# Softmax attention in a decoder kernel: the mask goes from TensorE to VectorE, and copies move from VectorE to ScalarE and GpSimd

## The chip, the cores and the metric

The kernel runs on one core of a Trainium2 chip. The metric is the device time of one launch in microseconds: the median of 3 runs is 2063.61 us (2063.49 to 2066.27). One further launch was recorded by the hardware profiler and is read below. Its engines are TensorE (PE in the rows; PEld are its weight loads), VectorE (DVE), ScalarE (ACT), GpSimd (POOL) and SyncE (SP), which issues transfers.

## The reference

A decoder of six sublayers works on 16 sequences of 128 tokens and 512 features. Each sublayer's result is added to x and layer-normed. The change touches the first and the fifth, both softmax attention over 16 heads of 32 features:

```python
# first: grouped queries (4 heads of k and v), rotary q and k
scores = jnp.einsum('btkgd,bskd->bkgts', qg, k) * scale
mask = jnp.tril(jnp.ones((T, T), dtype=scores.dtype))
scores = scores + mask[None, None, None]
p = jax.nn.softmax(scores, axis=-1)
out = jnp.einsum('bkgts,bskd->btkgd', p, v).reshape(B, T, C)
return out @ wo.T + bo
# fifth: causal, k and v from 128 latent features
scores = jnp.einsum('bhqd,bhkd->bhqk', qh, kh) * inv_sqrt_d
scores = jnp.where(causal, scores, jnp.finfo(scores.dtype).min)
attn = jax.nn.softmax(scores, axis=-1)
out = jnp.einsum('bhqk,bhkd->bhqd', attn, vh)
return out @ Wout.T
```

So in both a mask that is the same for all heads is added to 128 by 128 scores of each head: 0 and 1 in the first, 0 and a very low number in the fifth. The others are an attention over latents, a ternary feed-forward, a decayed attention without softmax and one with experts.

## The kernel before

`attention_phase` writes the code of the first ("gqa"), the fourth ("decay") and the fifth ("causal") sublayer; `soft` is true for the two with softmax, which run from about 10 to 270 us and from about 1297 to 1531 us of the profiled execution. A "batch" is one sequence: its 128 tokens are the 128 partitions. Products whose inputs need more exactness than one pass gives are made of three matmuls (L97 to L99): each factor is split into a rounded high part, written by ScalarE, and a low part, the difference.

The order of work is a list, `plan`, of events (name, batch, half or part). Each engine walks through that list and does its share of each event, so its order is fixed when the program is written; `act_plan` is ScalarE's own version of the list. The events are:

- S: the scores of a batch, all 16 heads in four PSUM banks. Before them TensorE writes the mask into each bank by a matmul with the identity (L857), and the scores are added to it (L866). For each half h (8 heads) VectorE takes the negated maximum (`nb`, L714) and ScalarE the exponentials out of PSUM into `pr`, with their sums (L572).
- T: TensorE turns the 8 probabilities' tiles of a half (L875), VectorE copies them to `pt` (L726).
- rec and rt: VectorE takes the reciprocals of the sums (L729), GpSimd spreads them over 512 columns (`spread`, L479), TensorE turns that (L880), ScalarE copies it to `rts` (L588).
- pv: probabilities by v (L891). VectorE multiplies the result by `rts` into `on` (L732), and ScalarE copies that to the high part `oth` (L592).
- lo: VectorE subtracts `oth` from `on` into the low part `otl` (L738).
- out: the output projection of `oth` and `otl` (12 matmuls), added to X by VectorE (L744), which then takes the statistics for the norm (L215 to L219). GpSimd makes the inverse root (L482).
- x, c, q, k, v: the turned inputs and the projections of the next group of 4 batches, split up over the "slots" of this group (two slots a batch, one in the middle of each of its halves). x and c have a high part by ScalarE (L540) and a low part by VectorE (L684); q, k and v are copied by VectorE (L688, L699, L704 or L710).
- mag: ScalarE sums absolute weights for the third sublayer (L578, first stage only); kr: a split for the second.

Projections, rt, pv and out share two PSUM banks in turn, so each needs the bank of the one before last to be copied out. TensorE's order in one batch b is: mask and scores of b, the first slot, T of half 1 of b-1, out of b-2, rt of b-1, the second slot, T of half 0 of b, pv of b-1. The last four batches have no slots to fill, since there is no next group.

## Time and profile before

| | |
|---|---|
| median of 3 runs | 2063.61 us |
| the profiled execution | 2068.66 us |
| its span, first to last instruction | 2066.9 us |
| mean granted TensorE clock | 0.97 |
| TensorE busy | 1886.0 us, 91% |
| VectorE busy | 1052.3 us, 51% |
| ScalarE busy | 708.4 us, 34% |
| GpSimd busy | 346.9 us, 17% |

A timeline row gives the start in us from the span's start, the duration in us, the engine, the line, the operation with output<-input, and in brackets how long the engine stood idle ahead of it and what ended that. Matmuls overlap in TensorE's pipeline, so the distance between starts says what one costs and the duration is longer. A wait for several things is put down to the last.

### The profile page before, as it was taken

The page shows a single profiled execution, that of the slowest core. Times are in us where ns is not written, and L with a number is a line of the kernel's source. Part 1 is how long each engine was busy: PE and PEld are TensorE (multiplying, and loading weights), DVE is VectorE, ACT ScalarE, POOL GpSimd, SP SyncE. Part 2 cuts the span into 40 slices and gives each one's busy share as a digit, 9 for nine tenths or more (in the row PEclk, how much of TensorE's full clock was granted, in tenths as well). Part 3 has the DMA queues.
Part 4 walks back from the last instruction along what each step waited for, and adds up shares of the span by engine and source line. Part 5 has one row for each costly group of instructions (what it writes and reads, how often), then busy time and mean ns, then how long its engine had stood idle before and what let it go on. Part 6 is the DMA issues. An engine that isn't in the chain of part 4 may idle for free. (4 is left out here: it accounts for less than half of the span.)

```text
span 2066.9 us, 32715 instructions
## 1 busy us (share of the span) xinstructions
PE 1886.0 (91%) x12124; PEld 1533.9 (74%) x12124; DVE 1052.3 (51%) x1852; ACT 708.4 (34%) x2276; POOL 346.9 (17%) x307
## 2 busy tenths in 40 slices
PE   8899888999999989999989999899979999999990
PEld 6666576788888867777767777677658877999990
DVE  4666854455455446433364457577765333222226
ACT  3555724344443332212141111455552121233322
POOL 1111100000000018100020010001103200735225
PEclk9999999999999999999999999899999999999995
DMA  7110143000000013000084000100013300643246
GB/s 240 43 40 21 43 149 95 1 1 1 1 1 1 1 55 114 1 0 0 0 314 181 1 1 32 42 1 1 1 47 126 129 1 16 239 165 126 76 128 193
DMA packets 65566, 135.83 MB, mean 66 GB/s; under 512 B 6672, under 2 KB 24976, under 8 KB 63376
## 3 DMA queue, kind: packets, MB, share of 16 engines
q1 hardware_dynamic: 41616, 96.24, 13.4%
q0 software_dynamic: 5840, 27.92, 3.9%
q10 hardware_dynamic: 17968, 9.71, 1.8%
q8 instruction: 96, 1.57, 0.3%
q14 instruction: 46, 0.38, 0.1%
HBM read 90.60 MB, written 43.25 MB: 65 GB/s over the span
## 5 line engine op out<-in xcount | busy, mean ns | idle before, releaser
L1472 PE MATMUL banks<-ternary_xth,ternary_wq 128*128 (+1 forms) x352 | 140.6, 399 | 5.0 <-DVE ternary_wq L1403 3.7
L1472 PE MATMUL banks<-ternary_xtl,ternary_wq 128*128 (+1 forms) x352 | 139.4, 396 | 0.0
L97 PE MATMUL banks<-latent_vh,latent_cth 128*128 128x512 f32 x256 | 104.2, 407 | 3.5 <-DVE latent_ctl L1173 3.5
L97 PE MATMUL banks<-weights,expert_xgh 128*128 x312 | 104.4, 335 | 2.3 <-DVE expert_xgl L2074 2.3
L572 ACT ACTIVATE gqa_pr<-banks,gqa_nb 128x128 f32<-128x128 f32 x256 | 90.1, 390 | 32.8 <-DVE gqa_nb L714 32.8
L99 PE MATMUL banks<-weights,expert_xgl 128*128 x312 | 101.2, 324 | 0.0
L98 PE MATMUL banks<-weights,expert_xgh 128*128 x312 | 101.1, 324 | 0.0
L572 ACT ACTIVATE causal_pr<-banks,causal_nb 128x128 f32<-128x128 f32 x256 | 90.0, 395 | 31.3 <-DVE causal_nb L714 31.2
L98 PE MATMUL banks<-latent_vl,latent_cth 128*128 128x512 f32 x256 | 100.3, 392 | 0.0
L99 PE MATMUL banks<-latent_vh,latent_ctl 128*128 128x512 f32 x256 | 100.1, 391 | 0.0
L1432 DVE TENSOR_TENSOR ternary_hf<-ternary_sg,banks 128x512 f32<-128x512 f32 x44 | 30.2, 687 | 135.4 <-issue 79.5
L1126 ACT ACTIVATE latent_pt<-banks 128x1024 f32<-128x1024 f32 x32 | 32.9, 1027 | 189.1 <-PE banks L1272 189.1
L1373 ACT ACTIVATE ternary_sg<-banks 128x512 f32<-128x512 f32 x44 | 26.3, 598 | 192.3 <-PE banks L1472 192.3
L1117 ACT ACTIVATE latent_pr<-banks,latent_nb 128x128 f32<-128x128 f32 x256 | 90.2, 373 | 0.0
L97 PE MATMUL banks<-latent_xgh,latent_ch 128*128 128x256 f32 x256 | 77.9, 304 | 9.4 <-DVE latent_xgl L1167 4.6
L1472 PEld LDWEIGHTS banks<-ternary_xth,ternary_wq 128*128 128x128 f32 x352 | 67.3, 191 | 23.2 <-DVE ternary_xtl L70 4.1
L1087 POOL TENSOR_TENSOR latent_rs<-latent_ve,mhalf 128x1 f32<-128x1 f32 x15 | 8.3, 550 | 445.8 <-DVE latent_ve L219 445.8
L1173 DVE TENSOR_TENSOR latent_ctl<-banks,latent_cth 128x512 fp32r<-128x512 f32 x64 | 42.9, 689 | 71.5 <-ACT latent_cth L1104 71.5
L1484 PE MATMUL banks<-ternary_wq,ternary_hh 128*128 128x512 f32 x176 | 70.9, 403 | 8.1 <-DVE ternary_hl L1436 5.8
L1472 PEld LDWEIGHTS banks<-ternary_xtl,ternary_wq 128*128 128x128 f32 x352 | 67.3, 191 | 14.2
L2082 DVE TENSOR_TENSOR expert_hf<-expert_sg,banks 128x352 f32<-128x352 f32 x39 | 20.4, 522 | 107.8 <-PE banks L99 107.8
L98 PE MATMUL banks<-latent_xgl,latent_ch 128*128 128x256 f32 x256 | 72.9, 285 | 0.0
(463 smaller groups left out, 5375.3 us busy)
## 6 DMA issues: line engine op xcount, KB each, us to landing
x_slots<-decay_zeros SPq DMA_DIRECT2D x39, 256.0 KB
y_slots<-decay_zeros SPq DMA_DIRECT2D x39, 256.0 KB
y_slots<-expert_ys SPq DMA_DIRECT2D x39, 256.0 KB
expert_xin<-x_slots SPq DMA_DIRECT2D x38, 256.0 KB, 2.9
weights_raw<-in_expert_experts SPq DMA_DIRECT2D x4, 2176.0 KB, 9.7
gqa_tw<-in_ternary_w ACTq DMA_DIRECT2D x4, 2112.0 KB
ternary_raw<-in_ternary_w SPq DMA_DIRECT2D x11, 768.0 KB, 4.3
expert_raw<-in_expert_experts POOLq DMA_DIRECT2D x3, 2176.0 KB, 9.8
```

Source lines behind the costliest of these rows:

```text
L97: pe.matmul(out, wh, xh, start=first, stop=False, **kw)
L98: pe.matmul(out, wh, xl, start=False, stop=False, **kw)
L99: return pe.matmul(out, wl, xh, start=False, stop=last, **kw)
L572: a = act.activation(pr[:, h, c, :], S.bank[2 * h + c // 4][:, (c % 4) * P:(c % 4 + 1) * P], ACT.Exp, bias=nb[:, h, c:c + 1], accum_out=su ...
L1117: a = act.activation(pr[:, c, :], S.bank[x][:, j * P:(j + 1) * P], ACT.Exp, bias=nb[:, c:c + 1], accum_out=sums[:, c:c + 1])
L1126: act.activation(pt[:, :, :], pair(1), ACT.Copy).then_inc(pt_done, 1)
L1173: dve.tensor_tensor(ctl[:, x, :], S.bank[2 + x], f32(cth[:, x, :]), ALU.subtract).then_inc(ct_lo, 1)
L1373: act.activation(sg[:, j % 2, :], gate[j % 2][:, :], ACT.Sigmoid).then_inc(sig_done, 1)
L1432: dve.tensor_tensor(hf[:, j % 2, :], sg[:, j % 2, :], up[j % 2][:, :], ALU.mult).then_inc(hf_done, 1)
L1472: a = pe.matmul(dst[:, :], wq[:, j, m, c * P:(c + 1) * P], x[:, c, toks], start=c == 0 and n == 0, stop=c == C - 1 and n == 1)
L1484: a = pe.matmul(yb[i][:, :], h[:, j % 2, i * P:(i + 1) * P], wq[:, j, 2, :], start=j == 0 and n == 0, stop=j == J - 1 and n == 1)
L2082: dve.tensor_tensor(hf[:, i % 2, :], sg[:, i % 2, :], up[i % 2][:, 0:F1], ALU.mult).then_inc(hf_done, 1)
```

## The change

In the two softmax stages:

1. The mask matmuls go, and with them `maskr` and `identr` and ScalarE's two copies that made them. VectorE adds the mask while it moves the scores of a half from PSUM to `pr` in SBUF (a 128x1024 addition, `masked`), and takes the maximum from there; ScalarE takes the exponentials in place in `pr`. TensorE's next scores wait for `masked` instead of for the exponentials.
2. T and rt of b-1 come directly behind the scores of b, ahead of the first slot; out of b-2 keeps its place between the slots. (In batch 1 they come behind the first slot.) The reciprocals come first in VectorE's batch.
3. ScalarE copies the second half's turned probabilities (`pt_late`), q, and in the fifth stage the even parts of v; its list has T and rt ahead of the exponentials, and the copies of a first slot's q or v between the two halves' exponentials.
4. The low part of the attention's output is made by GpSimd instead of VectorE. In the list it stands ahead of the spreading of the next batch's reciprocals.
5. In a batch with x in its first slot, and in batch 1, the second half's scores stay behind that slot.

```diff
@@ buffers @@
-            maskr, identr = sb("maskr", [P, P], F32R), sb("identr", [P, P], F32R)
+            mask = (S.tril if kind == "gqa" else S.causal)[:, :].unsqueeze(1).broadcast_to((P, 8, P))
@@ plan @@
         for b in range(B + 2):
             for h in range(2):
+                if soft and h == 0 and b >= 2:
+                    plan.append(("lo", b - 2, 0))
+                if soft and h == 0 and 1 <= b <= B:
+                    plan.append(("rec", b - 1, 0))
                 if b < B and (h == 0 or not soft):
                     plan.append(("S", b, h))
-                if soft and h == 0 and b >= 2:
-                    plan.append(("lo", b - 2, 0))
+                with_x = b % GT == 0 and b < B - GT
+                turned = [("T", b - 1, 1), ("rt", b - 1, 0)] if soft and h == 0 and 1 <= b <= B else []
+                if b != 1:
+                    plan += turned
+                if soft and h == 0 and b < B and not with_x and b != 1:
+                    plan.append(("S", b, 1))
                 if b < B - GT:
                     plan += [(n, b // GT + 1, i) for n, i in by_slot[2 * (b % GT) + h]]
...
+                if b == 1:
+                    plan += turned
-                if soft and h == 0 and b < B:
+                if soft and h == 0 and b < B and (with_x or b == 1):
                     plan.append(("S", b, 1))
...
-                    if h == 0 and 1 <= b <= B:
-                        plan += [("T", b - 1, 1), ("rec", b - 1, 0)]
                     if h == 0 and b >= 2:
                         plan.append(("out", b - 2, 0))
-                    if h == 0 and 1 <= b <= B:
-                        plan.append(("rt", b - 1, 0))
@@ who copies @@
+        def copied_by_act(e):
+            if kind == "causal" and e[0] == "v":
+                return e[2] % 2 == 0
+            return e[0] == "rt" or e[0] == ("q" if soft else "k")
...
-            while e[0] in ("x", "c", "nx", "nc") and act_plan[j - 1][0] in ("S", "lo"):
+            while (e[0] in ("x", "c", "nx", "nc") and act_plan[j - 1][0] in ("S", "lo") or
+                   e[0] in ("T", "rt") and act_plan[j - 1][0] == "S" or
+                   soft and e[0] in ("q", "v") and copied_by_act(e) and act_plan[j - 1][0] == "S" and act_plan[j - 1][2] == 1):
@@ GpSimd @@
+                elif what == "lo":
+                    pool.wait_ge(oth_done, b + 1)
+                    pool.tensor_tensor(out=otl[:, b % 2, :], in0=on[:, b % 2, :], in1=f32(oth[:, b % 2, :]),
+                                       op=ALU.subtract).then_inc(otl_done, 1)
@@ ScalarE @@
+                if what == "q" and e in act_frees:
+                    act.wait_ge(pp_full, place[e] + 1)
+                    ...
+                        act.activation(qt[:, b % 2, h, :], bank_of(e), ACT.Copy, scale=scale).then_inc(free_a, 1)
+                elif what == "v" and e in act_frees:
+                    act.wait_ge(pp_full, place[e] + 1)
+                    act.activation(v[:, b % 2, h, :], bank_of(e)[:, 0:vw], ACT.Copy).then_inc(free_a, 1)
+                elif what == "T" and h == 1:
+                    act.wait_ge(pt_full, 2 * b + 2)
+                    act.activation(pt[:, b % 2, 8:16, :], unit_banks(2), ACT.Copy).then_inc(pt_late, 1)
...
                     for c in range(8):
-                        a = act.activation(pr[:, h, c, :], S.bank[2 * h + c // 4][:, (c % 4) * P:(c % 4 + 1) * P], ACT.Exp,
-                                           bias=nb[:, h, c:c + 1], accum_out=sums[:, b % 2, 8 * h + c:8 * h + c + 1])
+                        a = act.activation(pr[:, h, c, :], pr[:, h, c, :], ACT.Exp, bias=nb[:, h, c:c + 1], accum_out=sums[:, b % 2, 8 * h + c:8 * h + c + 1])
@@ VectorE @@
                     dve.wait_ge(s_full, b + 1)
-                    dve.tensor_reduce(nb[:, h, :], unit_banks(h), AX, ALU.max, negate=True).then_inc(max_done, 1)
+                    if u >= 2:
+                        dve.wait_ge(pt_full, u - 1)
+                    ...
+                    dve.tensor_tensor(pr[:, h, :, :], unit_banks(h), mask, ALU.add).then_inc(masked, 1)
+                    dve.wait_ge(masked, u + 1)
+                    dve.tensor_reduce(nb[:, h, :], pr[:, h, :, :], AX, ALU.max, negate=True).then_inc(max_done, 1)
...
-                elif what == "lo":
-                    dve.wait_ge(oth_done, b + 1)
-                    dve.tensor_tensor(otl[:, b % 2, :], on[:, b % 2, :], f32(oth[:, b % 2, :]),
-                                      ALU.subtract).then_inc(otl_done, 1)
@@ TensorE @@
-                        pe.wait_ge(exp_done if soft else pt_done, u)
-                    if soft:
-                        for r in range(4):
-                            pe.matmul(S.bank[r], identr[:, :], maskr[:, :].unsqueeze(1).broadcast_to((P, 4, P)),
-                                      start=True, stop=False)
+                        pe.wait_ge(masked if soft else pt_done, u)
```

TensorE's instructions around one batch of the fifth stage (b is 7 here) stand so before: the turning of probabilities, their product with v, the masks, the scores, and the first row of the slot, which projects v.

```order
L875 MATMUL banks<-ident,causal_pr 128x128 x8
L891 MATMUL banks<-causal_pt,pair_v 32x128 x16
L857 MATMUL banks<-causal_maskr,causal_identr 128x512 x4
L866 MATMUL banks<-pair_kt,pair_qt 128x128 x16
L97 MATMUL banks<-pair_wkh,pair_wvh 128x512
```

And now, at the same place:

```order
L890 MATMUL banks<-ident,causal_pr 128x128 x8
L910 MATMUL banks<-causal_pt,pair_v 32x128 x16
L881 MATMUL banks<-pair_kt,pair_qt 128x128 x16
L890 MATMUL banks<-ident,causal_pr 128x128 x8
L895 MATMUL banks<-ident,causal_spread 128x128 x4
L97 MATMUL banks<-pair_wkh,pair_wvh 128x512
```

The masks are gone, and the other half's probabilities and the spread reciprocals (`causal_spread`) are turned ahead of the slot's projections.

ScalarE in the fifth stage, from the copy of `rts` of batch 1 to the exponentials of batch 4, before:

```order
L588 ACTIVATE causal_rts<-banks 128x512
L592 ACTIVATE causal_oth<-causal_on 128x512
L572 ACTIVATE causal_pr,causal_sums<-banks,causal_nb 128x128 x16
L588 ACTIVATE causal_rts<-banks 128x512
L540 ACTIVATE pair_xgh<-banks 128x4x128 x2
L592 ACTIVATE causal_oth<-causal_on 128x512
L540 ACTIVATE pair_xgh<-banks 128x4x128 x2
L572 ACTIVATE causal_pr,causal_sums<-banks,causal_nb 128x128 x16
```

And now, from the copy of `oth` of batch 1, behind the exponentials of batch 2 (L595 are exponentials, eight to a half):

```order
L614 ACTIVATE causal_oth<-causal_on 128x512
L586 ACTIVATE causal_pt<-banks 128x1024
L610 ACTIVATE causal_rts<-banks 128x512
L595 ACTIVATE causal_pr,causal_sums<-causal_pr,causal_nb 128x128 x8
L581 ACTIVATE pair_v<-banks 128x512
L595 ACTIVATE causal_pr,causal_sums<-causal_pr,causal_nb 128x128 x8
L581 ACTIVATE pair_v<-banks 128x512
L551 ACTIVATE pair_xgh<-banks 128x4x128 x2
L614 ACTIVATE causal_oth<-causal_on 128x512
```

The exponentials of batch 3 (the third row before; the fourth and sixth now) stand behind the two copies for batch 2, where before only the copy of `oth` of batch 1 was ahead of them, and a copy of v stands behind each half of them; `oth` of batch 2 comes behind all of these.

GpSimd in the fifth stage, three batches before:

```order
L482 TENSOR_TENSOR causal_rs<-causal_ve,mhalf 128x1
L479 COPY causal_spread<-causal_rec 128x512
L482 TENSOR_TENSOR causal_rs<-causal_ve,mhalf 128x1
L479 COPY causal_spread<-causal_rec 128x512
```

And now:

```order
L493 COPY causal_spread<-causal_rec 128x512
L500 TENSOR_TENSOR causal_rs<-causal_ve,mhalf 128x1
L496 TENSOR_TENSOR causal_otl<-causal_on,causal_oth 128x512
L493 COPY causal_spread<-causal_rec 128x512
L500 TENSOR_TENSOR causal_rs<-causal_ve,mhalf 128x1
L496 TENSOR_TENSOR causal_otl<-causal_on,causal_oth 128x512
```

Each spreading of reciprocals now has the low part of the batch before ahead of it, which reads `causal_oth`.

## Rows read from the trace of the kernel before

**Rows 1.** Busy time of each engine (part 1 of the page).

```profile
PE 1886.0 (91%) x12124; PEld 1533.9 (74%) x12124; DVE 1052.3 (51%) x1852; ACT 708.4 (34%) x2276; POOL 346.9 (17%) x307
```

**Rows 2.** Busy time by engine in a stretch of the first and of the fifth stage (windows); start:end, length, then per engine.

```profile
160.00:220.00 60.00, 53.73 (x392) 39.97 (x390) 42.38 (x68) 34.69 (x158) 7.36 (x10) 1.00 0.14 36
1380.00:1440.00 60.00, 55.97 (x498) 42.98 (x496) 45.30 (x77) 32.12 (x151) 5.81 (x9) 1.00 0.00 1
```

**Rows 3.** TensorE over one batch of the first stage (timeline); start, duration in us.

```profile
110.11 1.17 PE L866 MATMUL banks<-gqa_kt,gqa_qt 32*128 32x128 f32 x32
...
117.49 0.39 PE L99 MATMUL banks<-gqa_woh,gqa_otl 128*128 128x512 f32 x1
...
118.45 0.63 PE L880 MATMUL banks<-ident,gqa_spread 128*128 128x128 f32 x4 [0.57 <-POOL gqa_spread L479]
...
118.83 0.48 PE L97 MATMUL banks<-gqa_xgh,gqa_wqh 128*128 128x512 f32 x1
...
121.67 1.04 PE L875 MATMUL banks<-ident,gqa_pr 128*128 128x128 f32 x8
...
122.63 1.07 PE L891 MATMUL banks<-gqa_pt,gqa_v 128*32 128x512 f32 x8
...
123.63 1.20 PE L857 MATMUL banks<-gqa_maskr,gqa_identr 128*128 128x512 f32 x4
...
124.75 1.17 PE L866 MATMUL banks<-gqa_kt,gqa_qt 32*128 32x128 f32 x32
```

**Rows 4.** VectorE, ScalarE and GpSimd in the same batch (timeline).

```profile
111.36 1.23 DVE L714 TENSOR_REDUCE gqa_nb<-banks 128x8 f32<-128x1024 f32 x1 [1.43 <-PE banks L866]
...
112.62 0.37 ACT L572 ACTIVATE gqa_pr<-banks,gqa_nb 128x128 f32<-128x128 f32 x1 [2.03 <-DVE gqa_nb L714]
...
115.03 0.40 ACT L572 ACTIVATE gqa_pr<-banks,gqa_nb 128x128 f32<-128x128 f32 x1
...
118.70 0.68 DVE L216 BATCH_NORM_STATS2 gqa_six<-X 128x6 f32<-128x512 f32 x1
...
118.97 1.41 ACT L578 ACTIVATE gqa_tw<-gqa_tw 128x1408 f32<-128x1408 f32 x1
...
120.33 0.63 ACT L588 ACTIVATE gqa_rts<-banks 128x512 f32<-128x512 f32 x1
...
122.74 1.22 DVE L726 COPY gqa_pt<-banks 128x1024 f32<-128x1024 f32 x1
...
123.88 0.68 DVE L732 TENSOR_TENSOR gqa_on<-banks,gqa_rts 128x512 f32<-128x512 f32 x1
...
124.60 0.63 ACT L592 ACTIVATE gqa_oth<-gqa_on 128x512 fp32r<-128x512 f32 x1 [3.64 <-DVE gqa_on L732]
```

**Rows 5.** Durations of four operations over the whole run (by line); min/median/max in ns.

```profile
L479 POOL COPY gqa_spread<-gqa_rec x16: 608/776/779, 54.3 to 258.5; 128x512 f32<-128x512 f32 x16
L464 POOL TENSOR_TENSOR X<-X,gqa_bor x16: 1257/1272/1729, 14.9 to 160.3; 128x512 f32<-128x512 f32 x16
L717 DVE TENSOR_TENSOR decay_pt<-banks,decay_dec x32: 1211/1215/1224, 1081.3 to 1284.4; 128x1024 f32<-128x1024 f32 x32
L1126 ACT ACTIVATE latent_pt<-banks x32: 1024/1027/1030, 325.3 to 749.4; 128x1024 f32<-128x1024 f32 x32
```

**Rows 6.** TensorE where the next x is turned, first stage (timeline).

```profile
89.05 0.66 PE L808 MATMUL banks<-ident,X 128*128 128x128 f32 x4 [2.24 <-ACT gqa_rts L588]
```

**Rows 7.** TensorE in the fifth stage's beginning (timeline).

```profile
1321.00 1.08 PE L880 MATMUL banks<-ident,causal_spread 128*128 128x128 f32 x4 [3.76 <-POOL causal_spread L479]
...
1329.66 1.17 PE L866 MATMUL banks<-pair_kt,pair_qt 32*128 32x128 f32 x32
```

**Rows 8.** TensorE in the fifth stage's last batches (timeline).

```profile
1505.01 1.17 PE L866 MATMUL banks<-pair_kt,pair_qt 32*128 32x128 f32 x32
...
1523.56 0.47 PE L97 MATMUL banks<-pair_wkl,causal_oth 128*128 128x512 f32 x1 [2.29 <-DVE causal_otl L738]
```

**Rows 9.** The clock granted behind the first stage's last wait (windows).

```profile
258.00:262.00 4.00, 4.00 (x14) 3.11 (x13) 0.89 (x4) 0.00 (x0) 0.78 (x1) 0.62 0.00 0
```

More of the change, by code:

```diff
@@ L371, in attention_phase @@
         place = {e: k for k, e in enumerate(banked)}
-        by_act = [e for e in banked if e[0] == "rt" or kind == "decay" and e[0] == "k"]
+        by_act = [e for e in banked if copied_by_act(e)]
         by_dve = [e for e in banked if e not in by_act]
@@ L559, in _ @@
                         constants()
-                if what == "k" and e in act_frees:
+                if what == "q" and e in act_frees:
+                    act.wait_ge(pp_full, place[e] + 1)
+                    if kind == "gqa":
+                        act.wait_ge(biases_done, 1)
+                        act.activation(qt[:, b % 2, h, :], bank_of(e), ACT.Identity, bias=bqs[:, h:h + 1],
+                                       scale=scale).then_inc(free_a, 1)
+                    else:
+                        act.activation(qt[:, b % 2, h, :], bank_of(e), ACT.Copy, scale=scale).then_inc(free_a, 1)
[4 more added lines that the diff above has]
+                    act.wait_ge(pt_full, 2 * b + 2)
+                    if kind == "gqa" and b == 1:
+                        act.wait_ge(ws_lo, 3)
+                    act.activation(pt[:, b % 2, 8:16, :], unit_banks(2), ACT.Copy).then_inc(pt_late, 1)
+                elif what == "k" and e in act_frees:
                     act.wait_ge(pp_full, place[e] + 1)
@@ L684, in _ @@
                     dve.tensor_tensor(lo, four(bank), f32(hi), ALU.subtract).then_inc(free_d, 1)
-                elif what == "q":
-                    dst = qt[:, b % 2, h, :]
-                    if kind == "gqa":
-                        a = dve.tensor_scalar(dst, bank, bqk[:, h:h + 1], scale, ALU.add, ALU.mult)
-                    elif kind == "decay":
-                        a = dve.tensor_scalar(dst, bank, bqk[:, h:h + 1], None, ALU.add)
-                    else:
-                        a = dve.tensor_scalar(dst, bank, scale, None, ALU.mult)
-                    a.then_inc(free_d, 1)
+                elif what == "q" and e in dve_frees:
+                    dve.tensor_scalar(qt[:, b % 2, h, :], bank, bqk[:, h:h + 1], None, ALU.add).then_inc(free_d, 1)
                 elif what == "k" and e in dve_frees:
@@ L704, in _ @@
                     dve.tensor_copy(v[:, b % 2, :, :], four(bank)).then_inc(free_d, 1)
-                elif what == "v":
+                elif what == "v" and e in dve_frees:
                     dst = v[:, b % 2, h, :]
@@ L721, in _ @@
                     dve.tensor_tensor(S.ahead.krl[:, :], S.ahead.kr, f32(S.ahead.krh[:, :]), ALU.subtract).then_inc(kr_lo, 1)
-                elif what == "T":
+                elif what == "T" and h == 0:
                     dve.wait_ge(pt_full, u + 1)
@@ L731, in _ @@
                     dve.wait_ge(free_a, act_frees[("rt", b, 0)])
+                    if b >= 2:
+                        dve.wait_ge(otl_done, b - 1)
                     dve.tensor_tensor(on[:, b % 2, :], bank, rts[:, :], ALU.mult).then_inc(free_d, 1)
@@ L847, in _ @@
                         continue
-                    if u == 0 and soft:
-                        pe.wait_ge(const_hi, 2)
                     if u % 8 == 0 and not (kind == "causal" and b == 0):
@@ L864, in _ @@
                             dst = S.bank[r][:, j * P:(j + 1) * P]
-                            if soft:
-                                m = pe.matmul(dst, q, k, start=False, stop=j == 3)
-                            else:
-                                m = pe.matmul(dst, k, q, start=True, stop=True)
+                            lhs, rhs = (q, k) if soft else (k, q)
+                            m = pe.matmul(dst, lhs, rhs, start=True, stop=True)
                     m.then_inc(s_full, 1)
@@ L871, in _ @@
                     pe.wait_ge(exp_done, u + 1)
-                    if u >= 1:
-                        pe.wait_ge(pt_done, u)
+                    if h == 1:
+                        pe.wait_ge(pt_done, b + 1)
+                    elif b >= 1:
+                        pe.wait_ge(pt_late, b)
                     for c in range(8):
@@ L881, in _ @@
                 elif what == "pv":
-                    pe.wait_ge(pt_done, 2 * b + 2)
+                    if soft:
+                        pe.wait_ge(pt_done, b + 1)
+                        pe.wait_ge(pt_late, b + 1)
+                    else:
+                        pe.wait_ge(pt_done, 2 * b + 2)
                     if not (kind == "causal" and b < GT):
```

24 lines of the change are left out of this document (9 added, 15 removed).

## Prediction

> **What bounds the kernel now.** I read the page first: TensorE is busy 91% of the span and no other engine over 51% [rows 1]. The mean is over stages with other limits, so I then took windows of the two softmax stages: TensorE 53.7 and 56.0 us of 60, VectorE 42.4 and 45.3, ScalarE 34.7 and 32.1, at full clock [rows 2]. So here too TensorE is next to the bound, and what can be gained is work taken from it or a wait in its line. The timeline of one plain batch (a part of q in each slot) shows both. From scores to scores are 14.64 us (110.11 to 124.75) [rows 3]. Of these the masks take 1.12 (123.63 to 124.75). One wait stands in the line: the last matmul of the output projection starts at 117.49 and, at the pitch of these rows, is through 0.23 later; the turning of the spread reciprocals starts at 118.45, so 0.72 pass, released by GpSimd's spreading. Together 1.84 us a batch stand to be won, some 32 times.
>
> **The chain that the change makes.** I set the start of pv (probabilities by v of batch b-1, 122.63) to zero and follow the new order. VectorE's product with the reciprocals starts at 1.25 (123.88), since it stands behind a copy of 1.22, and is through at 1.93; ScalarE's high part runs from 1.97 to 2.60 [rows 4]. So far nothing is changed. GpSimd now makes the low part, and behind it in its order stands the spreading for the next batch. The nearest row for a 128x512 operation of two inputs on GpSimd is the addition of the bias, 1.27 us median; the spreading has 0.61 to 0.78 [rows 5]. That makes 2.65, 3.92, 4.52 with 0.61, and with the 0.14 that TensorE needs behind the spreading now (117.53 and 0.78 to 118.45 in the profile, 0.14) the turning starts at 4.66. Before, the spreading had only the reciprocals ahead of it and these were early; now it waits for the end of the batch before through GpSimd's order alone, not through data. What TensorE has in between is pv 1.00, the scores 1.11, the turning of the other half's probabilities 0.86 [rows 3]: 2.97. The new wait is 1.69 us, and behind it on TensorE stands all the rest of the batch, on ScalarE the copy `rts` and behind that the exponentials.
>
> The spreading's price is where a page bears on the case. The rows have 0.78 in most batches, beside VectorE's norm of X, and 0.61 at its least [rows 5]. After the change VectorE is at the mask addition or the maximum then, of one SBUF input each. The Trainium skill (GPSIMD Engine Reference, section Key points) says that GpSimd's SBUF interfaces are shared with VectorE and contend where VectorE runs in a 2-port mode or has two SBUF inputs. By that rule 0.61 holds after the change. If it were 0.78 the chain would be 4.83 and the sum 0.17 x 30 = 5 us higher; I keep that as an end of the range.
>
> **The plain batch.** 4.66, turning 0.39, slot 2.84, output projection 2.80, slot 2.76, turning of the first half 0.97: 14.42 against 14.64 now, 0.2 less. The 1.84 us removed are thus spent in the new wait. Each 0.1 us of the chain is 3 us over 30 batches; at a chain of 4.88 the plain batch is even.
>
> **What I cost at nothing there.** The mask addition: 1.215 us by the fourth stage's product of the same shape out of PSUM [rows 5]. VectorE has scores at 2.2, so addition and maximum end near 4.7, while ScalarE is free for the exponentials only behind `rts` at 4.66 + 0.39 + 0.63 = 5.7. The cover is 1.0 us; without it, half of what is over lands on T of the first half. ScalarE's copy of the other half's probabilities (1.03 us for this shape [rows 5]) runs from 3.1 to 4.1, ahead of `rts`. q on ScalarE (0.6) stands between the exponentials' halves, and T of the first half needs only the first. The exponentials read SBUF instead of PSUM: eight start 0.345 us apart now (112.62 to 115.03) [rows 4], and I take that unchanged, with 0.03 either way.
>
> **The rest of the first stage.** Its start: two small copies fewer on ScalarE, -0.3. Five plain batches -1.0. Batches 3 and 7 turn the next x in the second slot, and there TensorE waited 2.24 us for `rts`, which stood behind 1.41 us of absolute sums [rows 4, 6]; now `rts` is early. So 2.24 and the masks' 1.12 go, 1.69 comes, and I add 0.4 for the x parts, which ScalarE takes later: -1.3 each, -2.6. Batches 4 and 8, x in the first slot: -0.15 by the plain batch's sum and, as my estimate, 0.5 more for fewer matmuls at a low clock, -0.7 each, -1.4. The split for the second stage stands behind an exponential that is now later: +1.6. Batch 11, with a short v slot: -1.7, since nothing of x follows there and its wait for `rts` goes. The last four batches have no slots: there the loop is chain 4.66, turning 0.39, `rts` 0.65, exponentials 2.91, turning 0.97 and the release 0.15: 9.75 against 10.03, but with absolute sums behind the exponentials `oth` is late and the loop is 10.8. Entry +1.0, one loop -0.3, two +0.8, the end +1.6: +3.9. Sum of the stage: -0.3 - 1.0 - 2.6 - 1.4 + 1.6 - 1.7 + 3.9 = -1.5.
>
> **The fifth stage.** This is where the change costs.
> - Beginning: q and c of the next group and the split of the output weights stand on ScalarE now between or ahead of exponentials that TensorE awaits. TensorE already waits 3.76 us there [rows 7]. I get the scores of batch 2 (1329.66 now) 2.3 us later, and 1.3 in the next batch: +3.6.
> - Batches 3, 7 and 11, with v. Slot one writes v0 and v1 into the two banks in turn, and the output projection needs v0's bank. Before, VectorE copied it (0.68). Now ScalarE does, behind the first half's exponentials: these run from 5.7 to 8.6, the copy to 9.25. TensorE is there at 6.7. A wait of 2.5, and some more for the later v parts behind the second half's: +2.9 each, +8.7. With the copy between the exponentials' halves, T of the first half isn't touched. Its other end is 1.5, if the engine's next parts are absorbed.
> - Batches 6 and 10, k: VectorE's statistics (0.68 [rows 4], 1.3 with its small parts) come ahead of the first k copy and are later relative to it: +0.55 each, +1.1. Batches 4, 5, 8, 9: +1.9 together, from q and c on ScalarE.
> - The last batches: from the scores of batch 15 to its output projection are 18.55 us now, with a wait of 2.29 for `otl` [rows 8]. The new chain gives 20.6, since the output projection of batch 14 now stands between the turned reciprocals and pv and GpSimd's 1.27 replaces VectorE's 0.68. With entry +1.0 and three loops of -0.3: +2.2.
> Sum: 3.6 + 8.7 + 1.1 + 1.9 + 2.2 = +17.5.
>
> GpSimd against VectorE for the low part is the other place of a page: 1.27 against 0.68 [rows 4, 5]. The Trainium skill (GPSIMD Engine Reference, section Engine selection) has two-input elementwise operations about twice slower on GpSimd and advises VectorE. The rows agree with it. A low part at VectorE's price would make the chain 4.07, and the plain batch 0.6 shorter.
>
> **Sum.** -1.5 + 17.5 = +16.0 on the profiled execution's 2068.7 us gives 2084.7. That execution is 5.05 us above the median of the runs shown (2063.6), so the forecast against the runs is 2079.6; I take 2079.
>
> **Rivals.**
> - A, faster. The chain is shorter than I have it, because GpSimd's operations overlap VectorE's and ScalarE's better than their rows (0.61 and 1.27 are rough for this engine), or VectorE's order lets the product start at 0.7. The point from which it decides is a chain of about 4.1 us: then 30 batches gain 0.55 more each, -17 in all, and below that the 35.8 us of masks (32 x 1.12) come through. With 3.7 the sum is 16 - 29 = -13: 2051. For it: 1.84 us a batch are truly removed. Against: three of the four parts of the chain are rows of this same batch. Chance 0.15.
> - B, no change. The chain is as I have it, but v's copies cost 1.5 each and the beginning nothing, and the shorter x batches gain more: -1.5 + 17.5 - 4.2 - 3.6 - 6 = +2: 2066. Chance 0.10.
> - C, much slower. Each wait of TensorE can let the granted clock fall, as behind the first stage's last wait of about 3 us, where 0.62 is granted [rows 9]. Now every batch has a wait of 1.7. If it falls behind a third of them and matmuls of some 3 us run at half speed: +1.7 x 10 = +17 on top, 2096; in all of them, over 2120. Against: waits of 0.7 to 0.9 leave it at 1.00 now [rows 2]. Chance 0.12.
>
> **How the numbers follow.** A change of under 0.2%, 4.1 us, can't be told from none. My own case (2068 to 2093) has 0.63, A 0.15, B 0.10, C 0.12. Faster 0.15, within 0.2% 0.10, slower 0.75. The range takes in most of A's near side and of C's: 2058 to 2097.
>
> **What would show it.** In the new trace: the wait ahead of the turning of the spread reciprocals, in every batch, about 1.7 us, released by GpSimd; its spreading directly behind the low part. The scores' starts 14.4 apart in plain batches. In the fifth stage's batches 3, 7 and 11 a wait of 2.5 ahead of the output projection, released by ScalarE's copy of v. Wrong would be: no wait at the turning, or batches of 13 us; the granted clock below 0.95 in the two stages' middle; exponentials that wait for the maximum in the plain batch, which would make the mask addition dear.

## The result and the profile after

The changed kernel takes 2100.57 us (median of 4 runs, 2094.56 to 2105.52) against 2063.55 us (4 runs, 2059.03 to 2066.27): a ratio of 1.0173, 95% interval 1.0154 to 1.0193. It is 37 us slower. The forecast had the direction and less than half the size (2079, which is 15 slower, with a range up to 2097). The profiled execution is 2100.08 us, 31.4 above that of before, and its granted clock is 0.963 against 0.970.

The first part of the page, as in [rows 1]:

```profile
PE 1862.1 (89%) x11996; PEld 1519.9 (72%) x11996; DVE 1051.8 (50%) x1819; ACT 774.1 (37%) x2338; POOL 379.7 (18%) x339
```

TensorE is busy 24 us less, where the masks alone were 36 us (32 x 1.12), and it is busy a smaller share: it waits more, and what it still does takes longer. Windows from the scores of batch 0 to the next stage's first instruction, of both softmax stages, say where. The last three numbers of a row are the granted clock, the share of DMA and GB/s. Before:

```profile
37.23:271.73 234.50, 200.24 (x1481) 147.71 (x1481) 156.05 (x251) 133.38 (x579) 34.52 (x42) 0.97 0.14 38
1300.37:1533.27 232.90, 203.62 (x1866) 157.41 (x1865) 166.81 (x276) 119.82 (x558) 20.89 (x32) 0.96 0.03 8
```

After:

```profile
35.93:282.76 246.83, 193.54 (x1421) 145.59 (x1421) 157.96 (x240) 164.74 (x608) 51.64 (x59) 0.92 0.11 35
1310.25:1565.60 255.35, 191.26 (x1806) 150.32 (x1805) 168.41 (x261) 153.83 (x594) 38.56 (x49) 0.94 0.03 9
```

The two stages take 502.2 us for 467.4, 34.8 more; the rest of the program is 3 us shorter in this execution. If each window's length is multiplied by what its clock lacks to 1.00, the deficit is 234.5 x 0.03 + 232.9 x 0.04 = 16 us before and 246.8 x 0.08 + 255.4 x 0.06 = 35 us after. This counts time in which TensorE stands idle too, so it is no price yet. The busy times of the same rows give an estimate of one: 403.9 us before are 368.0 without the masks, and after the change the same matmuls take 384.8, some 17 us more. The lower clock is half speed in short stretches, as here behind a wait of 2.74 us, where matmuls of one shape start 0.42 us apart and a little later 0.23:

```profile
242.03 0.63 PE L895 MATMUL banks<-ident,gqa_spread 128*128 128x128 f32 x4 [2.74 <-POOL gqa_spread L493]
...
243.47 0.63 PE L97 MATMUL banks<-gqa_woh,gqa_oth 128*128 128x512 f32 x1
...
243.89 0.63 PE L98 MATMUL banks<-gqa_wol,gqa_oth 128*128 128x512 f32 x1
...
246.38 0.39 PE L98 MATMUL banks<-gqa_wol,gqa_oth 128*128 128x512 f32 x1
...
246.61 0.39 PE L99 MATMUL banks<-gqa_woh,gqa_otl 128*128 128x512 f32 x1
```

That had been a rival and not part of my sum.

TensorE over a plain batch of the first stage, against [rows 3]:

```profile
126.90 1.06 PE L910 MATMUL banks<-gqa_pt,gqa_v 128*32 128x512 f32 x8
...
127.89 1.17 PE L881 MATMUL banks<-gqa_kt,gqa_qt 32*128 32x128 f32 x32
...
129.00 1.09 PE L890 MATMUL banks<-ident,gqa_pr 128*128 128x128 f32 x8
...
131.54 0.63 PE L895 MATMUL banks<-ident,gqa_spread 128*128 128x128 f32 x4 [1.45 <-POOL gqa_spread L493]
...
137.26 0.39 PE L99 MATMUL banks<-gqa_woh,gqa_otl 128*128 128x512 f32 x1
...
140.21 1.04 PE L890 MATMUL banks<-ident,gqa_pr 128*128 128x128 f32 x8
...
142.18 1.17 PE L881 MATMUL banks<-gqa_kt,gqa_qt 32*128 32x128 f32 x32
```

And the chain beside it on the other engines, against [rows 4]:

```profile
127.01 1.22 DVE L749 COPY gqa_pt<-banks 128x1024 f32<-128x1024 f32 x1 [1.66 <-PE banks L890]
...
128.15 0.68 DVE L757 TENSOR_TENSOR gqa_on<-banks,gqa_rts 128x512 f32<-128x512 f32 x1
...
128.86 0.63 ACT L614 ACTIVATE gqa_oth<-gqa_on 128x512 fp32r<-128x512 f32 x1 [2.04 <-DVE gqa_on L757]
...
129.57 1.27 POOL L496 TENSOR_TENSOR gqa_otl<-gqa_on,gqa_oth 128x512 fp32r<-128x512 f32 x1 [3.59 <-ACT gqa_oth L614]
...
130.79 0.61 POOL L493 COPY gqa_spread<-gqa_rec 128x512 f32<-128x512 f32 x1
...
131.53 1.22 DVE L735 TENSOR_TENSOR gqa_pr<-banks,tril 128x1024 f32<-128x1024 f32 x1
```

This is the chain of the prediction, step by step: from the start of pv (126.90) the product starts at 1.25, the high part at 1.96, the low part at 2.67, the spreading at 3.89, and TensorE turns it at 4.64, where 4.66 was forecast. TensorE stood idle 1.45 for it, counted from the modelled end of its last turning; by the distances that the forecast used, which gave 1.69, it is 1.67 (4.64 less 2.97). The plain batch is 14.29 us (127.89 to 142.18), forecast 14.42, before 14.64.

What the sum lacked stands elsewhere. Long waits of TensorE in the changed kernel, one line for each place, in the order of time: the beginning of the first stage, a batch with x (two), the end of the first stage, the beginning of the fifth (two lines), and a batch with v (three like it):

```profile
55.99 0.80 PE L97 MATMUL banks<-gqa_xgh,gqa_wqh 128*128 128x512 f32 x1 [4.03 <-ACT gqa_qt L575]
...
92.37 0.86 PE L858 MATMUL banks<-ident,gqa_vt 128*128 128x128 f32 x4 [3.34 <-DVE gqa_xgl L707]
...
275.69 0.47 PE L97 MATMUL banks<-gqa_woh,gqa_oth 128*128 128x512 f32 x1 [3.78 <-POOL gqa_otl L496]
...
1331.16 1.43 PE L890 MATMUL banks<-ident,causal_pr 128*128 128x128 f32 x8 [4.19 <-DVE causal_pt L749]
...
1337.26 0.80 PE L97 MATMUL banks<-pair_xgh,pair_wqh 128*128 128x512 f32 x1 [3.81 <-ACT pair_qt L578]
...
1371.02 0.50 PE L97 MATMUL banks<-pair_wkl,causal_oth 128*128 128x512 f32 x1 [2.58 <-ACT pair_v L581]
```

### The profile page after: what moved, and what is told of

Its sections match the earlier page's. It is cut to its first block and busy times, and to the rows that moved or that the text cites. A ratio compares the mean times of both kernels' runs of the same rounds, so it can differ in the third digit from the quotient of the medians.

```text
span 2098.3 us, 32573 instructions
## 1 busy us (share of the span) xinstructions
PE 1862.1 (89%) x11996; PEld 1519.9 (72%) x11996; DVE 1051.8 (50%) x1819; ACT 774.1 (37%) x2338; POOL 379.7 (18%) x339
## 3 DMA queue, kind: packets, MB, share of 16 engines
q1 hardware_dynamic: 41616, 96.24, 13.2%
## 5 line engine op out<-in xcount | busy, mean ns | idle before, releaser
L595 ACT ACTIVATE causal_pr<-causal_pr,causal_nb 128x128 f32<-128x128 f32 x256 | 98.8, 390 | 7.8 <-DVE causal_nb L737 7.5
L595 ACT ACTIVATE gqa_pr<-gqa_pr,gqa_nb 128x128 f32<-128x128 f32 x256 | 98.8, 390 | 4.0 <-DVE gqa_nb L737 3.7
L765 DVE TENSOR_TENSOR X<-X,banks 128x512 f32<-128x512 f32 x48 | 33.0, 688 | 126.2 <-PE banks L99 126.2
```

Of the source, the lines that this page charges most:

```text
L595: a = act.activation(pr[:, h, c, :], pr[:, h, c, :], ACT.Exp, bias=nb[:, h, c:c + 1], accum_out=sums[:, b % 2, 8 * h + c:8 * h + c + 1])
L765: dve.tensor_tensor(row, row, bank, ALU.add).then_inc(free_d, 1)
```

## The experiments

Ten kernels ran. A median is of 4 to 10 runs, and the interval is that of the ratio to the kernel before; the last column is the length of both softmax stages in the profiled execution, as in the windows above. Medians of 4 runs whose intervals overlap are not told apart. Outside the two stages the profiled executions differ by up to 10 us, so a run's total and its last column need not move together.

| run | median, us | ratio to before | both stages, us |
|---|---|---|---|
| before | 2063.6 to 2065.2 | | 467.4 |
| changed | 2100.6 | 1.0154 to 1.0193 | 502.2 |
| e1 spreading first | 2057.4 | 0.9945 to 0.9980 | 459.9 |
| e2 low part on VectorE | 2064.8 | 0.9989 to 1.0010 | 467.9 |
| e3 reciprocals late | 2091.2 | 1.0094 to 1.0148 | 489.6 |
| e4 v on VectorE | 2096.2 | 1.0134 to 1.0188 | 500.1 |
| e5 filled waits | 2086.0 | 1.0087 to 1.0120 | 492.7 |
| e6 masks only | 2117.0 | 1.0237 to 1.0271 | 520.4 |
| e7 v first as well | 2044.9 | 0.9885 to 0.9918 | 447.2 |
| e8 orders mended | 2023.5 | 0.9777 to 0.9810 | 429.1 |
| e9 mended and filled | 2022.5 | 0.9777 to 0.9813 | 425.3 |
| e10 masks by matmul | 2062.4 | 0.9963 to 0.9999 | 467.0 |

**e1: the spreading ahead of the low part in GpSimd's order.** Two events of the plan change places:

```diff
+                if soft and h == 0 and 1 <= b <= B:
+                    plan.append(("rec", b - 1, 0))
                 if soft and h == 0 and b >= 2:
                     plan.append(("lo", b - 2, 0))
-                if soft and h == 0 and 1 <= b <= B:
-                    plan.append(("rec", b - 1, 0))
```

> The changed kernel, with the spreading of the reciprocals ahead of the low part in GpSimd's order; nothing else moves. Theory 1 (the change's loss is the chain pv, product, high part, low part, spreading, which TensorE awaits through GpSimd's order alone): the wait of 1.45 us ahead of the turned reciprocals goes in every plain batch (14.28 to about 12.85), the tail's loops get 1.1 shorter, and stretches at the lower clock behind those waits go too: 30 to 45 us less than the changed kernel, about 2055 to 2070. Theory 2 (ScalarE, which now has q, half of the turned probabilities and half of v beside the exponentials, is what TensorE awaits): the wait only moves to another place, at most 10 us less, above 2090.

It is 43 us faster than the changed kernel and faster than the one before. GpSimd and TensorE in a plain batch of it:

```profile
120.56 1.06 PE L910 MATMUL banks<-gqa_pt,gqa_v 128*32 128x512 f32 x8
...
121.56 1.17 PE L881 MATMUL banks<-gqa_kt,gqa_qt 32*128 32x128 f32 x32
...
122.71 0.61 POOL L493 COPY gqa_spread<-gqa_rec 128x512 f32<-128x512 f32 x1 [3.07 <-DVE gqa_rec L752]
...
123.28 1.28 POOL L496 TENSOR_TENSOR gqa_otl<-gqa_on,gqa_oth 128x512 fp32r<-128x512 f32 x1
...
123.59 0.60 PE L895 MATMUL banks<-ident,gqa_spread 128*128 128x128 f32 x4
```

The spreading starts 0.05 behind the last of the scores' matmuls, released by VectorE's reciprocals, the low part behind it, and TensorE turns the reciprocals without a wait; the output projection comes 3 us later, when the low part is long there. The plain batch is 12.63 us. So theory 1 holds: the whole loss of 37 us, and 6 more, hung on the order of two instructions on the engine that is 18% busy.

**e2: the low part on VectorE again**, behind the first half's mask and maximum.

```diff
-                elif what == "lo":
-                    pool.wait_ge(oth_done, b + 1)
-                    pool.tensor_tensor(out=otl[:, b % 2, :], in0=on[:, b % 2, :], in1=f32(oth[:, b % 2, :]),
+                elif what == "lo":
+                    dve.wait_ge(oth_done, b + 1)
+                    dve.tensor_tensor(otl[:, b % 2, :], on[:, b % 2, :], f32(oth[:, b % 2, :]),
```

> The changed kernel, with the low part of the output on VectorE again, behind the first half's mask and maximum in its order. Theory 1: the spreading is early as in the run above, so the same gain, 30 to 45 us less than the changed kernel; the low part comes later (at about 5.4 us behind the start of pv instead of 3.9), which the plain batch hides and the last batches don't, so it is 2 to 6 us above the run above. Theory 2: at most 10 us less.

36 us faster than the changed kernel, 7 slower than e1, where 2 to 6 were expected. The plain batches are the same 12.64; the last batches of the first stage are 11.69, 9.95 and 9.92 for 9.87, 9.02 and 9.44 in e1, and 10.86, 9.93, 11.49 for three of 9.04 in the fifth. The low part is worth moving to the slower engine, if nothing stands behind it.

**e3: the reciprocals turned at their old place.**

```diff
-                turned = [("T", b - 1, 1), ("rt", b - 1, 0)] if soft and h == 0 and 1 <= b <= B else []
+                turned = [("T", b - 1, 1)] if soft and h == 0 and 1 <= b <= B else []
...
                         plan.append(("out", b - 2, 0))
+                    if h == 0 and 1 <= b <= B:
+                        plan.append(("rt", b - 1, 0))
```

> The changed kernel, with the turning of the spread reciprocals at its old place, behind the output projection; GpSimd makes the low part ahead of the spreading as in the change. Theory 1: the chain of 4.64 us ends before TensorE comes to that place (6.5 us and more), so the wait is hidden: 20 to 40 us less than the changed kernel; ScalarE's copy of them is then behind the exponentials. Theory 2: ScalarE isn't relieved by this, no gain, within 5 us of the changed kernel.

Only 9 us: under the 20 to 40 of theory 1, over the 5 of theory 2. The wait for the spreading is gone and the plain batch is 13.50, but ScalarE's copy is now behind the exponentials, and others wait for that: 3.57 us ahead of x in batch 3, 1.6 ahead of the k projections, and the v wait grew from 2.58 to 3.89:

```profile
90.36 0.66 PE L831 MATMUL banks<-ident,X 128*128 128x128 f32 x4 [3.57 <-ACT gqa_rts L612]
...
1351.00 0.50 PE L97 MATMUL banks<-pair_wvh,pair_wkh 128*128 128x512 f32 x1 [1.59 <-ACT causal_rts L612]
...
1363.01 0.50 PE L97 MATMUL banks<-pair_wkl,causal_oth 128*128 128x512 f32 x1 [3.89 <-ACT pair_v L583]
```

In the plain batch the spreading is through 4 us before it is turned, so GpSimd's order doesn't matter there, and the early place of the reciprocals is of use in itself (12.63 in e1 for 13.50 here). With the chain out of the way and ScalarE's copy late, the waits pass on to ScalarE's order, which is theory 2's mechanism in this kernel, if not in the changed one.

**e4: all of v on VectorE.** `copied_by_act` loses its two lines on v.

> The changed kernel, with all parts of v in the fifth stage copied by VectorE again. The wait of 2.58 us ahead of the output projection in the three batches with v, which is put down to ScalarE's copy of v, should go: about 2.3 to 3 us each with the clock's fall behind it, 7 to 9 us less than the changed kernel. If another wait stands right behind it (VectorE's copy of v1, or its place behind mask and maximum), 2 us or less.

4.3 us between the medians, half of what was expected, and no more than the scatter: its runs (2093.2 to 2100.6) overlap those of the changed kernel (2094.6 to 2105.5). The profiled execution shows where it goes. The three batches with v get 1.1, 2.7 and 1.7 us shorter (16.64, 18.21, 15.06 to 15.56, 15.56, 13.41), 5.4 together; another batch grew from 15.24 to 16.60, at a granted clock of 0.90 for 1.00, and the end of the stage by 1.5. So in this execution the clock fell in another place than before; that the missing wait moved it there isn't shown.

**e5: waits filled with useless work.**

```diff
                 elif what == "rt":
+                    for j in range(12 if b >= 1 else 0):
+                        pe.transpose(bank[:, (j % 4) * P:(j % 4 + 1) * P], S.ident[:, :], S.ident[:, :])
                     pe.wait_ge(spread_done, b + 1)
...
                     if soft:
+                        for j in range(30 if b == B - 1 else 0):
+                            pe.transpose(bank[:, (j % 4) * P:(j % 4 + 1) * P], S.ident[:, :], S.ident[:, :])
                         pe.wait_ge(otl_done, b + 1)
```

> The changed kernel, with twelve more turnings of the identity (0.12 us each) by TensorE into the bank it writes next, ahead of each wait for the spread reciprocals, and thirty ahead of the last batch's wait of 3.8 us in both stages. They do no useful work and are overwritten; the waits they fill were idle. Theory C (part of the loss is not the waits themselves but the lower clock behind them: the deficit, span times one minus granted clock over the batches, is about 25 us in the changed kernel and 11 in the one before): the clock in the last batches of the first stage (0.85 now in two of them) and behind the last waits is 1.00, and the kernel is 5 to 12 us faster, though it does more. Without that theory: no change, or up to 5 us slower where the fill is longer than the wait.

14.6 us faster than the changed kernel, with 420 more matmul instructions on TensorE and nothing else changed. The last batches of the first stage go from 11.66, 10.67, 11.70 (granted 0.85, 1.00, 0.85) to 11.14, 10.02, 11.28, all at 1.00, and from the scores of batch 15 to the next stage it is 29.9 for 34.0 us. The deficit goes from 35 to 239.6 x 0.04 + 253.1 x 0.05 = 22 us. Work was added and none taken away, so this shows that the lower clock is a cause of its own. Its size is less sure: of the 14.3 us between the two profiled executions 9.5 lie in the two stages (492.7 for 502.2), 5.7 of them at the stages' ends, and 4.5 between the stages, where nothing was filled (1023.0 us for 1027.5; the other runs have 1025 to 1032 there). So the fills are worth about 10 us of the 37, up to 15 if the rest is theirs too, and they reach only the waits that I filled.

**e6: the kernel before with the masks' move alone** (part 1 of the change; the diff is that of the change's buffers, VectorE, exponentials and TensorE parts).

> The kernel before, with part 1 of the change alone: masks added by VectorE into SBUF, maximum and exponentials from there, no mask matmuls; all orders and copies as before. If the masks are worth their 1.12 us a batch where nothing else moves: plain batches from 14.64 to about 13.5 and 25 to 35 us less than before, about 2035. If VectorE, which then has 12.7 us of work in a batch, becomes what TensorE awaits (its copies behind two additions of 1.2 us): plain batches at 14 to 15 and within 8 us of before. The copies that the change took from VectorE would then be what makes the masks' move pay.

52 us slower than before, the worst of all, though TensorE lost 1.12 us of work a batch. VectorE and what waits for it:

```profile
149.11 1.03 PE L863 MATMUL banks<-ident,gqa_pr 128*128 128x128 f32 x8
...
150.25 1.22 DVE L708 TENSOR_TENSOR gqa_pr<-banks,tril 128x1024 f32<-128x1024 f32 x1
...
151.51 1.22 DVE L710 TENSOR_REDUCE gqa_nb<-gqa_pr 128x8 f32<-128x1024 f32 x1
...
152.65 1.21 DVE L722 COPY gqa_pt<-banks 128x1024 f32<-128x1024 f32 x1
...
154.31 0.68 DVE L740 TENSOR_TENSOR X<-X,banks 128x512 f32<-128x512 f32 x1
...
155.00 0.63 PE L868 MATMUL banks<-ident,gqa_spread 128*128 128x128 f32 x4 [2.11 <-DVE X L740]
```

Mask addition, maximum and copy stand in a row, 1.2 us each; the addition of the second half may not write `pr` before the old probabilities are turned, so the row starts late, and behind it stand the reciprocals and the addition to X, whose bank the turned reciprocals need. TensorE waits 2.11 us there in nearly every batch with slots, and the granted clock is 0.90 in nearly every plain batch, 16.6 us long. VectorE is busy 72% there (43.27 of 60 us from 155 to 215), 2 points more than before (41.81). So the masks' move alone doesn't pay, for the order of VectorE's work and not for its sum. Which of the other parts makes it pay (the copies taken from VectorE, or the new order) isn't shown: no run has one of them without the other.

**e7: e1, and ScalarE copies v0 ahead of the exponentials.**

```diff
-                   soft and e[0] in ("q", "v") and copied_by_act(e) and act_plan[j - 1][0] == "S" and act_plan[j - 1][2] == 1):
+                   soft and e[0] == "v" and copied_by_act(e) and act_plan[j - 1][0] == "S" or
+                   soft and e[0] == "q" and copied_by_act(e) and act_plan[j - 1][0] == "S" and act_plan[j - 1][2] == 1):
```

> The run with the spreading first (2057.4 us), with ScalarE's copy of v0 in the fifth stage ahead of the first half's exponentials instead of behind them. The wait of 2.71 us ahead of the output projection in batches 3, 7 and 11 goes, and nothing else waits, since v0 is there before the maximum: 6 to 9 us less than that run. If the two banks or the later v parts hold it up again: under 3 us.

12.4 us less than e1, where 6 to 9 were expected; the three batches went from 18.07 (granted 0.81), 16.85 (0.90), 14.07 to 14.07, 14.07, 11.92, all at 1.00: 8.9 us for three waits of 2.7. The rest lies in other batches (1.9 us in the first stage), and this run can't tell it from scatter (e1's runs lie within 7 us).

**e8: the other orders.** On top of e7:

```diff
+        dve_plan = list(plan)
+        if soft:
+            for i in (3, 2):                      # x's low parts ahead of the first mask addition
+                dve_plan.remove(("x", 1, i))
+                dve_plan.insert(dve_plan.index(("S", 0, 0)), ("x", 1, i))
...
+            ahead_of(("q", 1, 1), ("S", 1, 0))    # in act_plan
+            for b in (3, 7, 11):
+                if kind == "causal":
+                    ahead_of(("v", b // GT + 1, 2), ("S", b, 1))
+                for i in range(2):
+                    ahead_of(("x", b // GT + 2, i), ("S", b, 1))
```

The second half's exponentials of batch 0 stand directly behind the first's, the output weights are split behind the first turned probabilities, and VectorE makes the last low part.

> The run with the spreading and v0 first, and besides: in batch 0 VectorE makes x's low parts ahead of the mask addition; ScalarE has both halves' exponentials of batch 0 and the second q of batch 1 where TensorE wants them; the split of the fifth stage's output weights comes behind the first turned probabilities; in batches 3, 7 and 11 x and v2 are copied ahead of the second half's exponentials; the very last low part is VectorE's. The waits of 3.0, 3.6, 3.9 (twice) in the first stage and of 3.5, 4.2, 3.8 in the fifth get under 1.5 each, and the stretches below full clock there end: 15 to 30 us less than the run with the spreading first, about 2030 to 2042, faster than the kernel before by 1 to 1.7%. If these waits are only passed on to the next one, it is above 2050.

2023.5 us, 41 less than before (0.9793), 77 less than the changed kernel: below the range I gave. Batches 3 and 7 of the first stage are 13.2 us for 18.1 in e1, batches 0 to 2 of the fifth 44.6 for 49.2, and the granted clock is 0.98 in the first stage and 0.96 in the fifth. (The profiled execution was the slowest of the four, 2031.4.) Several orders changed at once here, so no single one of them has its price shown by the total. It is the fastest whose gain is clear; e9 can't be told from it.

**e9: e8 with 25 turnings of the identity ahead of the last batch's wait.**

> The run with the orders mended (2023.5 us), with 25 more turnings of the identity by TensorE ahead of the last batch's wait of 3.2 us in both softmax stages; they do no useful work. If the clock behind that wait was what the filled run gained there, the last output projection and what follows run at full clock: 2 to 5 us less, 2018 to 2022. If the gain of the filled run came from the waits inside the batches alone: within 1.5 us of 2023.5.

1 us less than e8, inside the scatter of both. The ends did get shorter, from 29.1 and 29.4 us (scores of batch 15 to the next stage) to 26.7 and 27.8, but the run shown has a fall to 0.88 in another batch, which cost 1.6. So it can't say whether this last wait's clock was part of e5's gain.

**e10: e7 with the masks as matmuls again** (maximum and exponentials read PSUM, TensorE's scores wait for the exponentials).

> The run with the spreading and v0 first (2044.9 us), with part 1 of the change undone: the masks are matmuls again, maximum and exponentials read PSUM. If removing the masks' 1.12 us a batch is worth its price once the copies are spread and no wait hides it, this is 32 x 1.12 = 36 us slower and somewhat more, since TensorE's scores wait for the exponentials again: 2080 to 2095. If the maximum, which then is ready 1.2 us sooner, gives that back in the last batches: 2060 to 2075. Below 2050 the masks' move is worth nothing even here.

17.5 us slower than e7: half of the masks' 36, and inside the range (2060 to 2075) that I had given to the case in which the last batches give some back. They don't: a last batch is 10.5 for 9.0, and the plain batch 13.77 for 12.64, so there the masks' 1.12 are there in full. What gives some back are the beginnings, where the mask addition stands ahead of x (the first two batches of the first stage take 25.2 for 27.6), and batches of the fifth stage that come out only 0.2 to 0.6 longer. And it is level with before: all of parts 2 to 5, with the two orders mended, gain 0.2% without the masks' move.

## Why the prediction was wrong

The direction held: slower was given 0.75. The size did not: +16 in the profile's terms, 31 in the profiled execution, 37 in the medians (and 2100.6 is above the range's end at 2097). The mechanism that was forecast is there, and the step that failed is the sum over the batches that aren't plain, together with the clock that was left out of it. The first stage, with its start, was put at -1.5 and came out at +11.0; the fifth at +17.5 and came out at +22.5; the rest was 2.1 shorter.

- The chain through GpSimd's order was right to 0.02 us, with each of its parts, and with the plain batch (0.35 gained for 0.2). The wait was 1.67 for 1.69 by the same measure. e1 shows that the wait at its end is the chain's alone.
- The spreading's price: 0.612 us median after, where [rows 5] had 0.776. The rule on the shared interfaces (the Trainium skill, GPSIMD Engine Reference, section Key points) agrees with this: beside the mask addition (in e1) and the maximum, of one SBUF input each, it has its short time. That its long time comes beside VectorE's scaling of X because of a 2-port mode isn't shown by a row.
- The wait for v0: 2.58 us, forecast 2.5; the batches of the fifth stage from 3 to 11 came to 11.3 us more, forecast 11.7.
- Wrong: "-1.3 each" for batches 3 and 7 of the first stage. They are 0.5 longer each. The wait for `rts` went as I said, but behind it one of 3.3 us came, for x's low part: x's high part is on ScalarE behind the second half's exponentials and 1.36 us of absolute sums. I had priced that at 0.4. e8 moves it ahead of them, and e1's 18.1 becomes 13.2.
- Wrong: the last batches of the first stage, "+3.9". From batch 12 it is 11.1: three loops 1.6, 0.6 and 1.7 longer and the end 7.2. The output projection now stands directly ahead of the turning, so VectorE's addition and statistics come ahead of its copy and product. Behind the pv ahead of batch 15's scores the product starts at 2.23 and not at 1.25, and the turned reciprocals wait 2.10 for that chain:

```profile
247.80 1.06 PE L910 MATMUL banks<-gqa_pt,gqa_v 128*32 128x512 f32 x8
...
248.90 1.22 DVE L749 COPY gqa_pt<-banks 128x1024 f32<-128x1024 f32 x1
...
250.03 0.68 DVE L757 TENSOR_TENSOR gqa_on<-banks,gqa_rts 128x512 f32<-128x512 f32 x1
```

  The loop before it has the absolute sums (1.37 us) ahead of the high part and the wait of 2.74 shown above, with half speed behind it. In e5, with its waits filled, the end is 4.0 us shorter at full clock: so more than half of its 7.2 is the clock's.
- Too small: batch 5 of the first stage, whose chain the split for the second stage, late in batch 4, holds up. It was put at +1.6 and is 3.1 longer (17.75 for 14.64), at a granted clock of 0.90; at full clock in e5 it is 16.09, near the +1.6.
- Too small: the beginnings. The first two batches of the first stage took 1.9 more, priced at nothing, and the first three of the fifth 7.8 more, priced at +3.6. Waits of 3.0 to 4.2 us stand there. e8's new orders at these places bring both beginnings down.
- The clock was a rival (chance 0.12, 2096) beside my case and should have been a term of it. The busy times put it at some 17 us, as an estimate, and e5 gives back 10 to 15. These aren't on top of the batches above but part of their lengths. I had also read [rows 9] wrongly: they don't lie behind the stage's last wait of about 3 us, but behind one of 1.83, and the last one, 2.29 long, left the clock at 1.00 (128x512 matmuls 0.43 apart behind the first, 0.23 behind the second). The trace before:

```profile
257.32 0.47 PE L97 MATMUL banks<-gqa_woh,gqa_oth 128*128 128x512 f32 x1 [1.83 <-DVE gqa_otl L738]
...
258.45 0.63 PE L97 MATMUL banks<-gqa_woh,gqa_oth 128*128 128x512 f32 x1
...
258.88 0.63 PE L98 MATMUL banks<-gqa_wol,gqa_oth 128*128 128x512 f32 x1
...
266.05 0.47 PE L97 MATMUL banks<-gqa_woh,gqa_oth 128*128 128x512 f32 x1 [2.29 <-DVE gqa_otl L738]
...
266.36 0.40 PE L98 MATMUL banks<-gqa_wol,gqa_oth 128*128 128x512 f32 x1
...
266.59 0.40 PE L99 MATMUL banks<-gqa_woh,gqa_otl 128*128 128x512 f32 x1
```

- The exponentials out of SBUF: taken as unchanged at 0.345 apart [rows 4]. They are 0.384 apart, seven distances in 2.69 us, ahead of the copy of v0 for which TensorE waits:

```profile
1367.32 0.39 ACT L595 ACTIVATE causal_pr<-causal_pr,causal_nb 128x128 f32<-128x128 f32 x1
...
1370.01 0.39 ACT L595 ACTIVATE causal_pr<-causal_pr,causal_nb 128x128 f32<-128x128 f32 x1
...
1370.39 0.58 ACT L581 ACTIVATE pair_v<-banks 128x512 f32<-128x512 f32 x1
```

That is past the 0.03 that I allowed by 0.01. It counts where TensorE awaits a half of them: eight distances, so 0.3 us each time as an estimate, in the last batches.

Rival A (a shorter chain and a gain by the masks) is not what this kernel does. e1 shows what a chain off TensorE's path gives, 2057 where I had 2051 for A, but by another order and not, as A had it, by operations that overlap.

## What to carry to other kernels

When work is moved to an idle engine, follow what stands behind it in that engine's order: a 1.3 us operation put ahead of a 0.6 us one cost more here than the 36 us of matmuls that the change saved. Draw such a chain from rows; it can be right to hundredths, and then draw the same for the batches that are not plain (first, last, those with an extra load), since the miss lay there: 7.2 in the last batches, 3.6 with x, 1.9 and 4.2 in the beginnings, 17 us against the 15 by which the profiled execution missed my sum, the rest being small terms of both signs. And give the new waits of TensorE a second price, the half speed that can follow. The length of a wait alone doesn't tell whether it follows. In the changed kernel it came behind a wait of 1.42 in batch 2 of the fifth stage (0.55 granted from 1348.72 to 1352.50) and not behind the same wait of 1.45 in the plain batches of the first; of the three waits of 2.6 for v it came behind the second alone (0.59 from 1433.37 to 1437.40). So carry it as a term with a range, and find in the trace which waits bring it.

## What the runs showed of the hardware that I had not expected

- Filling TensorE's waits with useless matmuls made a kernel 14.6 us faster, 9.5 of it inside the two stages that were filled.
- Half speed came behind a wait of TensorE of 1.83 us and not behind one of 2.29, 9 us later in the same execution.
- The exponentials with a sum of 128x128 start 0.384 us apart from SBUF and 0.344 from PSUM [rows 4], though single ones take 0.39 in both at the median. The instruction that reads the sum is 0.226 long with PSUM and 0.189 with SBUF. Why the distances differ isn't shown.
- GpSimd's copy of 128x512 has 0.612 us beside VectorE's mask addition or maximum, and 0.776 beside VectorE's scaling of X of 0.45 us.
